# Graph layer with attention and cell: gated rows stored in two pieces, and half of the input tiles turned by VectorE after a trip through DRAM

## What is computed

```python
xn = _layernorm(x)
u  = xn @ root + bias + sum_r mean_r(xn[src]) @ weight[r]        # r in 0..7
z  = concat([u, xn]) @ w_gate + b_gate
h  = tanh(u) * z + xn * (1 - z)
q, k = elu(xn @ Wq) + 1, elu(xn @ Wk) + 1 ; v = xn @ Wv ; g = sigmoid(xn @ Wg + bg)
mix = ((q * scale) @ (k.T @ v)) / clip(q . sum(k)) * g @ Wo      # per head
x = x + h + mix
f, i, o, c = gates(_layernorm(x)) ; out = x + o * tanh(i * c)    # from a zero state
```

## Time and profile before

| what | value |
|---|---|
| time, median of 3 runs | 2176.11 us (2174.67 to 2179.6) |
| time of the profiled execution | 2176.12 us |
| its span | 2174.2 us |
| TensorE busy | 2156.9 us, 99% |
| VectorE, ScalarE, GpSimd busy | 1220.6, 441.1, 721.2 us |
| DMA | 437.58 MB, mean 201 GB/s |

### The profile page before, as it was taken

One profiled execution on the slowest core, in us unless ns is written; L12 is line 12 of the kernel. 1 busy time (PEld: TensorE's weight loads), 2 busy tenths in 40 slices (PEclk: granted clock), 3 DMA queues, 4 the chain that ended last, 5 costly groups with the idle time before them and its releaser, 6 DMA issues.

```text
span 2174.2 us, 25191 instructions
## 1 busy us (share of the span) xinstructions
PE 2156.9 (99%) x9802; PEld 1746.0 (80%) x9802; DVE 1220.6 (56%) x1648; ACT 441.1 (20%) x618; POOL 721.2 (33%) x631
## 2 busy tenths in 40 slices
PE   8999999999999999999999999999999999999999
PEld 6878888888888888888777778889987888888887
DVE  6332678736666656576666567763355658534233
ACT  3221111211111111100221211112232313321121
POOL 4103002055555555554646445541221353000000
PEclk9999999999999999999999999999999999999999
DMA  7543321447788988783968878864169988604102
GB/s 253 192 133 94 111 86 48 134 165 239 236 292 287 315 294 295 248 304 101 337 232 297 283 269 297 302 203 158 68 184 267 281 286 268 179 15 132 55 29 80
DMA packets 216338, 437.58 MB, mean 201 GB/s; under 512 B 37320, under 2 KB 68501, under 8 KB 216219
## 3 DMA queue, kind: packets, MB, share of 16 engines
q1 hardware_dynamic: 145146, 239.60, 33.4%
q0 software_dynamic: 65248, 191.13, 26.7%
q10 hardware_dynamic: 5824, 5.25, 1.0%
HBM read 363.07 MB, written 113.90 MB: 219 GB/s over the span
## 4 chain that ended last, share of the span: by engine, by line
PE 97%; DMA 2%; DVE 1%; ACT 0%; SPq 0%; issue 0%; DVEq 0%; ACTq 0%
PE acc L1014 90%; PE acc L1009 5%; PE agg L947 1%; PE misc L932 1%; DMA bias_sb<-xs_d 1%; DMA o_d<-og 0%; DMA og<-o_d 0%; PE tp L896 0%; DVE Wlo L1207 0%; DMA xr<-in_x 0%; PE agg L1022 0%; PE acc L1022 0%; SPq L576 0%; DVE stats L1255 0%; DVE aTraw L1223 0%
## 5 line engine op out<-in xcount | busy, mean ns | idle before, releaser
L1014 PE MATMUL acc<-Whi,aThi 128*128 128x512 f32 (+1 forms) x2872 | 1137.1, 396 | 4.5 <-DVE aTlo L1217 3.0
L1014 PE MATMUL acc<-Whi,aTlo 128*128 128x512 f32 (+1 forms) x2872 | 1132.7, 394 | 0.0
L1014 PE MATMUL acc<-Wlo,aThi 128*128 128x512 f32 (+1 forms) x2872 | 1129.5, 393 | 0.0
L1014 PEld LDWEIGHTS acc<-Whi,aThi 128*128 128x128 f32 (+1 forms) x2872 | 533.2, 186 | 135.8 <-issue 3.4
L1014 PEld LDWEIGHTS acc<-Whi,aTlo 128*128 128x128 f32 (+1 forms) x2872 | 533.4, 186 | 133.0
L1014 PEld LDWEIGHTS acc<-Wlo,aThi 128*128 128x128 f32 (+1 forms) x2872 | 534.3, 186 | 131.4
L1814 POOL DMA_INDIRECT ring<-y_d,edge x390 | 486.2, 1247 | 426.2 <-DVE U L1439 157.3
L1207 DVE TENSOR_TENSOR Wlo<-Wraw,Whi 128x1024 fp32r<-128x1024 f32 x152 | 185.7, 1225 | 312.7 <-ACT Whi L1033 312.2
L1049 ACT COPY res<-acc 128x512 f32<-128x512 f32 (+1 forms) x180 | 105.7, 587 | 833.7 <-PE acc L1014 810.2
L1439 DVE SCALAR_TENSOR_TENSOR U<-ring,edge,U 128x1024 f32<-128x1024 f32 x180 | 230.2, 1279 | 22.7 <-DMA ring<-y_d,edge 22.5
L1439 DVE SCALAR_TENSOR_TENSOR odd<-ring,edge,odd 128x1024 f32<-128x1024 f32 x170 | 217.5, 1280 | 25.4 <-DMA ring<-y_d,edge 25.2
(11 more groups left out here) (183 smaller groups left out, 1052.1 us busy)
## 6 DMA issues: line engine op xcount, KB each, us to landing
y_d<-res SPq DMA_DIRECT2D x144, 256.0 KB
Wraw<-in_L_gnn_weight SPq DMA_DIRECT2D x64, 512.0 KB, 5.9
Wraw<-in_L_gnn_w_gate SPq DMA_DIRECT2D x16, 512.0 KB, 7.2
ring<-y_d,edge POOLq DMA_INDIRECT x390, 6.4
xr<-in_x SPq DMA_DIRECT2D x9, 512.0 KB, 4.3
xn_d<-xnb SPq DMA_DIRECT2D x9, 512.0 KB, 5.3
xs_d<-xr SPq DMA_DIRECT2D x9, 512.0 KB, 5.6
ur_d<-res SPq DMA_DIRECT2D x18, 256.0 KB
```

Source lines behind the costliest of these rows:

```text
L1014: mm = nc.tensor.matmul(to, a[:, k, rows(i)], b[:, s % 2, k, :], start=start, stop=stop)
```

## The change

Two edits.

**The gated rows in two pieces.** `store_o(g, last)` stores a group's first three quarters of the columns when two of the four pairs of the second half are gated, and the last quarter when all four are.

**The input's tiles 5 to 9.** They are no longer turned by TensorE. They are normalised into `xnb` as before, stored to `xn_d`, loaded back by quarters into `zx` (two slots, `load_z`), turned by VectorE and split like the gated rows. `TURN_AT` has new places for tiles 6 to 9. As the inner places of `aThi` now stand by quarters for all tiles, every weight is permuted on the host. For tiles 0 to 4 VectorE writes the normalised rows permuted into `zx`, TensorE turns them from there, and ScalarE copies them in the plain order into `xnb` (`copy_xn`), behind its rounding of the same tile; the store to `xn_d` and GpSimd's sum wait for that copy. SyncE's `x_rows` is split in `store_xn` and `store_xs`, with places of their own for tiles 5 to 9. Two semaphores go and their counts are kept by others (`codes_st`, `z_turned`).

```diff
-TURN_AT = {1: 1, 3: 2, 5: 3, 7: 4, 8: 5, 9: 6, 10: 7, 11: 8, 12: 9}
+TURN_AT = {1: 1, 3: 2, 5: 3, 7: 4, 8: 5, 10: 6, 11: 7, 12: 8, 13: 9}
+TURNED_BY_PE = 5
...
-STORE_O_AT = {place(Q_, 1, 6): 0, place(Q_, 1, 10): 1, place(O_, 0, 2): 2}
+STORE_O_AT = {place(Q_, 1, 5): (0, 0), place(Q_, 1, 6): (0, 1), place(Q_, 1, 9): (1, 0), place(Q_, 1, 10): (1, 1),
+              place(O_, 0, 0): (2, 0), place(O_, 0, 2): (2, 1)}
...
-            def store_o(g):
-                sp.wait_ge(gated, reads_to(12 + 4 * g + 3))
...
+            def store_o(g, last):
+                sp.wait_ge(gated, reads_to(12 + 4 * g + (3 if last else 1)))
+                cols = slice(3 * QUARTER, D) if last else slice(0, 3 * QUARTER)
...
-            def x_rows(t):
-
-                sp.wait_ge(ln_done, with_halves(t))
+            def store_xn(t):
+
+                if t < TURNED_BY_PE:
+                    sp.wait_ge(xn_copied, t + 1)
+                else:
+                    sp.wait_ge(ln_done, with_halves(t))
                 sp.dma_start(xn_d[rows(t), :], xnb[0:width(t), t % XS, :]).then_inc(xn_st[t % XS], 16)
+
+            def store_xs(t):
+
                 sp.wait_ge(xs_made, t + 1)
                 sp.dma_start(xs_d[rows(t), :], xr[0:width(t), t % XS, :]).then_inc(xs_st[t % XS], 16)
...
+            def load_z(t):
+
+                sp.wait_ge(xn_st[t % XS], 16 * (t // XS + 1))
+                if t - 2 < TURNED_BY_PE:
+                    sp.wait_ge(x_turned, with_halves(t - 2))
+                    sp.wait_ge(xn_copied, t - 1)
+                else:
+                    sp.wait_ge(z_turned, x_turnings(t - 2))
+                load_quarters(zx[:, t % 2, :], xn_d, t, z_in[t % 2])
...
             for q in range(UNITS + 1):
-                if q in TURN_AT:
-                    x_rows(TURN_AT[q])
-                if q in LN_AT and 2 <= LN_AT[q] < T - XS + 2:
+                if TURN_AT.get(q, T) < TURNED_BY_PE:
+                    store_xn(TURN_AT[q])
+                    store_xs(TURN_AT[q])
+                if q in LN_AT and LN_AT[q] < 7:
                     next_x(LN_AT[q] - 2)
+                if TURNED_BY_PE <= q - 3 < T:
+                    load_z(q - 3)
+                if TURNED_BY_PE <= q - 2 < T:
+                    store_xn(q - 2)
+                if TURNED_BY_PE <= q - 4 < T:
+                    store_xs(q - 4)
+                if q == 10:
+                    next_x(5)
...
+            def copy_xn(t):
+                act.wait_ge(ln_done, with_halves(t))
+                if t >= XS:
+                    act.wait_ge(xn_st[t % XS], 16 * (t // XS))
+                    act.wait_ge(xs_made, t - XS + 1)
+                nc.scalar.copy(by_quarters(xnb[:, t % XS, :]), by_steps(zx[:, t % 2, :])).then_inc(xn_copied, 1)
...
+                    if k == 4 and TURN_AT.get(q, T) < TURNED_BY_PE:
+                        copy_xn(TURN_AT[q])
...
+            def turn_x(t):
+                dve.wait_ge(z_in[t % 2], x_quarters_in(t))
+                turn_quarters(zx[:, t % 2, :], t, z_turned)
...
+                    if k == 2 and TURNED_BY_PE <= TURN_AT.get(q, 0):
+                        turn_x(TURN_AT[q])
...
-                pool.wait_ge(ln_done, with_halves(t))
+                if t < TURNED_BY_PE:
+                    pool.wait_ge(xn_copied, t + 1)
+                else:
+                    pool.wait_ge(ln_done, with_halves(t))
```

More of the change, by code:

```diff
@@ L298, in build @@
         assert e_at + 10048 <= M + 44512
+        zx = at(M + 45312, "zx", [128, 2, D])
+        assert M + 53504 <= end
         nodes = at(M + 44512, "nodes", [128, T], I32)
@@ L371, in build, with by_quarters, by_steps @@
         misc = ctx.enter_context(nc.psum_tensor("misc", [128, H], F32))
+        def by_quarters(a):
+            return a.rearrange("p (a j f) -> p j a f", a=4, f=32)
+        def by_steps(a):
+            return a.rearrange("p (j a f) -> p j a f", a=4, f=32)
         def turned_rows(w):
@@ L394, in build @@
         place_const, run_made, runs_in = sem("place_const"), sem("run_made"), sem("runs_in")
-        key_made, key_st, keys_in, ranked, held_made, tabled = (
-            sem(n) for n in ("key_made", "key_st", "keys_in", "ranked", "held_made", "tabled"))
+        key_made, keys_in, ranked, held_made, tabled = (
+            sem(n) for n in ("key_made", "keys_in", "ranked", "held_made", "tabled"))
         sent = [sem(f"sent{h}") for h in range(2)]
@@ L473, in quarters_in, with x_turnings, x1_turnings, x_quarters_in @@
             return 16 * sum(quarter_transfers(p) for p in range(t % places, t + 1, places))
+        def x_turnings(t):
+            return t - TURNED_BY_PE + 1
+        def x1_turnings(t):
+            return T - TURNED_BY_PE + t + 1
+        def x_quarters_in(t):
+            return 16 * sum(quarter_transfers(p) for p in range(t, TURNED_BY_PE - 1, -2))
         def blocks(a):
@@ L688, in load_o @@
                 if t == 3 * g:
-                    sp.wait_ge(rows_st, 16 * (4 if g == 2 else g + 1))
+                    sp.wait_ge(rows_st, 16 * (8 if g == 2 else 2 * g + 2))
                 if t >= 2:
@@ L904, in turn_x @@
                             tr = nc.tensor.transpose(tp[:, h, (k % 4) * 128:(k % 4) * 128 + 128],
-                                                     xnb[:, 0, k * 128:(k + 1) * 128], ident[:, :])
+                                                     zx[:, 0, k * 128:(k + 1) * 128], ident[:, :])
                         tr.then_inc(x_turned, 1)
@@ L909, in turn_x @@
                 pe.wait_ge(x_lo, with_halves(t - 1))
-                turn_rows(lambda k: xnb[0:width(t), t % XS, k * 128:(k + 1) * 128], width(t)).then_inc(x_turned, 1)
+                turn_rows(lambda k: zx[:, t % 2, k * 128:(k + 1) * 128], 128).then_inc(x_turned, 1)
             def any_bad():
@@ L954, in beside @@
                 kind, _, h = STAGE[s]
-                if q in TURN_AT and k == 2:
+                if TURN_AT.get(q, T) < TURNED_BY_PE and k == 2:
                     turn_x(TURN_AT[q])
@@ L1156, in _ @@
                 hi_w(n)
+            copy_xn(0)
             for q in range(UNITS + 1):
@@ L1210, in lo_x @@
             def lo_x(t):
+                if t >= TURNED_BY_PE:
+                    lo_turned(t, x_hi, with_halves(t), x_lo)
+                    return
                 dve.wait_ge(x_hi, with_halves(t))
@@ L1264, in ln_x @@
                 chain(nc.vector.tensor_tensor(y, y, work, ALU.mult))
-                if t >= XS:
+                if t >= TURNED_BY_PE:
                     dve.wait_ge(xn_st[t % XS], 16 * (t // XS))
                     dve.wait_ge(xs_made, t - XS + 1)
-                    dve.wait_ge(x_turned, with_halves(t - XS))
-                for part in ((half(0), half(1)) if t == 0 else (slice(0, D),)):
-                    nc.vector.tensor_scalar(xnb[0:w, t % XS, part], xr[0:w, t % XS, part], stats[0:w, 12:13], y,
+                    nc.vector.tensor_scalar(xnb[0:w, t % XS, :], xr[0:w, t % XS, :], stats[0:w, 12:13], y,
                                             ALU.subtract, ALU.mult).then_inc(ln_done, 1)
+                    return
+                if t >= 2:
+                    dve.wait_ge(x_turned, with_halves(t - 2))
+                    dve.wait_ge(xn_copied, t - 1)
+                for j in ((slice(0, 4), slice(4, 8)) if t == 0 else (slice(0, 8),)):
+                    nc.vector.tensor_scalar(by_steps(zx[:, t % 2, :])[:, j, :, :], by_quarters(xr[:, t % XS, :])[:, j, :, :],
+                                            stats[:, 12:13], y, ALU.subtract, ALU.mult).then_inc(ln_done, 1)
             def edge_order():
@@ L1956 @@
     turned = ("L0_ffn_W_i", "L0_ffn_W_o", "L0_ffn_W_c")
-    by_quarters = ("L0_gnn_w_gate", "L0_mix_Wo") + turned
+    by_quarters = ("L0_gnn_weight", "L0_gnn_root", "L0_gnn_w_gate", "L0_mix_Wq", "L0_mix_Wk", "L0_mix_Wv", "L0_mix_Wg",
+                   "L0_mix_Wo") + turned
     nc = bacc.Bacc("TRN2", target_bir_lowering=False, num_devices=1)
```

35 lines of the change are left out of this document (20 added, 15 removed).

## The result

The changed kernel takes **2186.18 us** (median of 6 runs, 2184.51 to 2190.67) against 2179.01 (6 runs on the same chip): a ratio of 1.0041, 95% interval 1.0031 to 1.0051. It is slower by 0.4%. The profiled execution took 2185.22 us, its span (first to last instruction) is 2183.4 against 2174.2 before, +9.2. By the medians the change costs 7.2 us: the profiled execution of the kernel before, 2176.12, lies 2.9 us under its median. What follows compares profiles.

A forecast was written before the change was run, and what follows sets the result against it. TensorE, busy 2156.9 of 2174.2 us, was taken to bound the kernel. From 2176.1, less 4.2 (transposes) and 3.0 (gated rows), plus 12.5 (late tiles) and 2.3 (clock), came 2183.7 us, range 2175.0 to 2190.5.

The forecast's parts named there:

- The transposes: First stage, TensorE: five groups of eight transposes, tiles 5 to 9, go from the bounding engine, saving 4.2 us.
- The gated rows: Start of stage O: an earlier first piece removes TensorE's whole 3.0 us wait for `aTlo`; bounds 0 and 3.0.
- The chain to tile 5: First stage: tile 5's copy, sum, landings, quarter load and turning make unit 10 wait 4.5 us, from 73.2 to 77.7.
- The first four steps: Start of tile 5's path: tile 4 rounded at 58.9, copied by 59.9, summed by 62.3, its sums landed at 65.2.
- The chain to tile 6: First stage: tile 6 turned behind tile 9's normalisation and load; unit 12 is 12.5 us late, the 4.5 contained.
- The clock: After unit 12's wait, about 11 TensorE matmuls run at half clock, costing 2.3 us once; bounds 0 and 2.3.
- What costs nothing: ScalarE's five copies, VectorE's five turnings, 2.4 MB more loads and piecewise writes of tiles 0 and 1: 0 us.
- The sum: Whole kernel: 2176.1 - 4.2 - 3.0 + 12.5 + 2.3 = 2183.7 us.
- the small delay: Rival: landings near 2.9 us or an early tile 9 load, TensorE loses 3 to 9 us, no measurable change; chance 0.22.
- the hidden round trips: Rival: tiles 5 and 9 come in time, TensorE never waits in the first stage, faster at 2168.9 us; chance 0.08.
- the gated rows bring nothing: Rival: something else in the full stretch keeps tile 8 late, 2186.7 us; chance 0.08 within the forecast's 0.70.

The follow-up runs named there:

- Experiment 8: The kernel of experiment 3 with tile 6's turning in iteration 9, ahead of tile 9's normalisation on VectorE: 2169.55 us, 0.9962 of the kernel before.
- experiment 3: The changed kernel with SyncE's queue reordered: tile 5's and 6's stores and quarter loads ahead, tile 9's load in iteration 8: 2171.28 us, 0.9972 of the kernel before.
- experiment 1: The kernel before with only the gated rows stored in two pieces: 2174.67 us, 0.9987 of the kernel before.
- experiment 4: The changed kernel with tile 9's normalisation moved behind tile 6's turning on VectorE, SyncE as it was: 2178.68 us, 1.0007 of the kernel before.
- Experiment 6: The changed kernel with unread extra matmuls ahead of units 10 and 12: 22 and 22 took 2186.96 us, 22 and 37 took 2183.51 us.
- experiment 7: The changed kernel with only tile 9 turned by VectorE, tiles 5 to 8 back on TensorE with permuted writes and copies: 2178.85 us, 1.0007 of the kernel before.
- experiment 5: The changed kernel with only tile 5's store to `xn_d` moved ahead of tile 4's stores on SyncE's queue: 2183.51 us, 1.0028 of the kernel before.
- experiment 2: The changed kernel with the gated rows stored in one piece again, so the input's edit alone: 2188.75 us, 1.0050 of the kernel before.
- experiment 9: The kernel before and the changed kernel, both unchanged, profiled a second time: spans 2178.6 us and 2185.6 us.

## Why the prediction was right

It said 2183.7 us, 2175.0 to 2190.5, slower; it is 2186.18, and 2185.22 for the profiled execution to which the sum was made. That the total fits has some luck in it: the sum took its base and its 3.0 us from one execution of the kernel before, whose median later was 2179.01, and that wait changes from one execution to the next. By its own steps:

- **The transposes, -4.2.** Right. The transposes of tiles 1 to 4 still take 0.87 to 0.89 us each, those of tiles 5 to 9 are gone. Experiment 8, without waits in the first stage, reaches stage Q 4.3 us ahead of before, and experiment 3, with one of 1.65, 2.3 us (1488.0).
- **The gated rows, -3.0.** Right in size, not in kind. Against the first profile the changed kernel gained 3.2 behind stage Q, on average over profiles the wait is 2.9 shorter, and the medians of experiment 1 differ by 3.6; but it was given as "the whole wait as gone", and the wait is anything from 0 to 4.1 us with two pieces, and 3.0 to 4.8 in the three profiles with the whole store. That the 3.0 was near the average is luck. The first piece went out at the time foretold (1606.17 in experiment 1), the loads 3.9 us earlier instead of 2.6; `bias_sb` still holds VectorE.
- **The chain to tile 5, +4.5.** The first four steps hold within 0.2 us (copy at 60.0, sum 62.5, landed 65.1). The step that was too small is the landing of tile 5's own store: 2.9 and 0.9 for the load ahead of it were assumed, 5.23 it took. The wait was 5.8.
- **The chain to tile 6, 12.5 in all.** Of the four landings two were taken at 3.8 and took 4.0 and 3.7; tile 9's load was issued at 84.8 (83.4) and took 5.85 (6.2). Normalising, turning and splitting took 7.3 us (7.2). Unit 12 came at 97.92 against a due time of 84.3: 13.6. The excess of 1.1 is the 1.3 us of tile 5's landing, handed down, less 0.3 on tile 9's load. That tile 6 hangs on tile 9's load is shown by experiment 4.
- **The clock, +2.3.** Right in mechanism, paid once as it said, and 2.9 us in size, since fourteen matmuls went slow and not eleven. Experiment 6 gives it by itself, 2.8. Its ground that a wait of 3.0 us costs nothing more doesn't carry over: 2.12 and 2.83 us (experiments 7 and 5) had a slow stretch.
- **What costs nothing.** The permuted write of tile 1 takes 0.81 us as before, the two halves of tile 0 1.00 together, as before. The 1.27 us that it took as a price for pieces was the write beside GpSimd (experiment 7). The copies stayed hidden in this change, apart from the one of tile 4, which the sum had on its path. That they are free in general is wrong: experiment 7.
- **The sum.** 2176.12 - 4.2 - 3.0 + 13.6 + 2.9 = 2185.4, measured 2185.22.

The rivals fell: the small delay needed five short landings, and the five were 2.6, 5.2, 4.0, 3.7 and 5.9 us; the hidden round trips needed SyncE free of tile 4's sums, and experiment 3, which frees it, is nearly that case, at 2171.28 with 1.65 us of wait left. That the gated rows bring nothing is ruled out by experiment 1's interval, 0.9978 to 0.9996.

## What to carry to other kernels

In this kernel a trip through DRAM (2.6 to 5.2 us for a store to land, 4.6 for the load by quarters) was cheap in itself, and dear in order: what cost was a queue that waited for a landing while unrelated transfers stood behind it. Walk the issuing engine's list and ask at each wait what stands behind it, then do the same for the engine that consumes; here two such places cost 16.7 us at stage Q (1502.7 against 1486.0 in experiment 8), and moving them made of a 0.4% loss a 0.4% gain. A wait seen once in a full stretch of transfers is a sample: profile again before counting its removal.

## What the runs showed of the hardware

- **The clock and standing.** TensorE stood 3.0 us in the earlier trace rows and 2.8 us at O in experiment 2 without a slow stretch; 3.7 us (experiment 6), 3.95 (experiment 9), 5.4 and 5.8 us each had one, of 7 to 14 matmuls, but so had 2.83 us (experiment 5) and 2.12 us (experiment 7). The length of the wait alone doesn't decide. In experiment 8 it stood 4.12 us, ran three matmuls at full distance and only then fell (timeline of TensorE):

```profile
1655.27 0.47 PE L1083 MATMUL acc<-Whi,aThi 128*128 128x512 f32 x1 [4.12 <-DVE aTlo L1302]
1655.58 0.39 PE L1083 MATMUL acc<-Wlo,aThi 128*128 128x512 f32 x1
...
1656.40 0.63 PE L1083 MATMUL acc<-Wlo,aThi 128*128 128x512 f32 x1
```

  In these runs the waits of 3.7 to 5.8 us cost their own length and 1.4 to 2.9 us more.
- **VectorE beside GpSimd.** In the changed kernel too: while GpSimd runs three sums from 60.09 to 67.21, two tiny steps of tile 7's normalisation take 1.66 and 2.14 us instead of 0.22 and 0.16. One ends at 64.86, the other at 67.22; the second sum ends at about 64.84 (an estimate, two thirds of the 7.12 us), the third at 67.21. Nobody waited for tile 7 there.

```profile
60.09 7.12 POOL L1866 TENSOR_TENSOR xr<-xr,xnb 128x1024 f32<-128x1024 f32 x3 [9.60 <-ACT xnb L1106]
...
63.20 1.66 DVE L1341 SCALAR_TENSOR_TENSOR stats<-stats 128x1 f32<-128x1 f32 x1
...
65.08 2.14 DVE L1343 TENSOR_TENSOR stats<-stats 128x1 f32<-128x1 f32 x1
```

- **The granted clock.** Around these waits it reads 0.50 where matmuls are 0.427 us apart, while in the first unit it reads 1.00 at the same distance (kernel before, columns as in the earlier trace rows). Read the distances as well.

```profile
11.00:13.00 2.00, 2.00 (x6) 1.60 (x5) 2.00 (x3) 1.31 (x2) 0.00 (x0) 1.00 1.04 389
```
